# Four graph layers on one core: GpSimd copies the next chunk's gather indices a column at a time, between its own indirect DMAs

## The reference, cut to what matters

```python
def _gat_layer(x, src, dst, W, a_s, a_d, b, heads, outc):
    h = (x @ W).reshape(N, heads, outc)
    e = leaky_relu(alpha_s[src] + alpha_d[dst], 0.2)       # alpha_s needed at src of every edge
    p = exp(e - segment_max(e, dst)[dst])
    alpha = p / (segment_sum(p, dst)[dst] + 1e-16)
    return segment_sum(h[src] * alpha[:, :, None], dst) + b
x = layernorm(x + GAT(GAT(x)))           # two GAT layers: stages g1 and g2
x = layernorm(x + GCN(x))                # two GCN layers: stages c1 and c2
x = layernorm(x + sheaf(x))              # per edge an MLP of x[src], x[dst]; sums at src and at dst
x = layernorm(x + product(x))            # messages summed at src
```

## Time and profile before

| what | us |
|---|---|
| median of 3 runs | 38449.33 |
| the runs | 38229.62, 38449.33, 38707.31 |
| the profiled execution, its own time | 38408.23 |
| its span, first to last instruction | 38406.5 |

### The profile page before, as it was taken

The page is one execution under the profiler, slowest core; times in us unless marked ns, Lnnn a source line. Parts: engine busy times, 40 slices in busy tenths (PEclk is TensorE's granted clock), DMA queues, the critical chain, the costliest instruction groups (busy, mean ns, idle before and its releaser), DMA issues. The chain is left out here.

```text
span 38406.5 us, 266237 instructions
## 1 busy us (share of the span) xinstructions
PE 14357.5 (37%) x71326; PEld 10765.9 (28%) x71326; DVE 16060.9 (42%) x34560; ACT 2592.4 (7%) x3901; POOL 22432.8 (58%) x20450
## 2 busy tenths in 40 slices
PE   1111110111111047665566613433434344166664
PEld 1110000101010036554455612222223222044443
DVE  2332237223232546774566713332333344244443
ACT  0000000000000000000000000100101000033330
POOL 5777761355555256663676645755675665477773
PEclk5555555555555567776787856666666666577775
DMA  2011113111111311111111110000000000200001
GB/s 45 13 13 12 12 12 115 24 19 21 19 21 19 102 37 28 29 29 18 25 30 29 28 9 11 10 12 9 10 12 9 10 12 9 54 15 15 13 15 48
DMA packets 1089229, 935.10 MB, mean 24 GB/s; under 512 B 580668, under 2 KB 1031892, under 8 KB 1063892
## 3 DMA queue, kind: packets, MB, share of 16 engines
q1 hardware_dynamic: 440100, 695.25, 6.2%
q0 software_dynamic: 646368, 201.76, 6.1%
q10 hardware_dynamic: 1872, 28.29, 0.2%
HBM read 497.08 MB, written 426.83 MB: 24 GB/s over the span
## 5 line engine op out<-in xcount | busy, mean ns | idle before, releaser
L1139 POOL DMA_INDIRECT messages<-se_M,se_rstage x2625 | 3090.6, 1177 | 2987.9 <-DVE se_M L1502 2193.8
L1139 POOL DMA_INDIRECT messages<-pe_M,pe_rstage x2625 | 3131.6, 1193 | 1098.1 <-issue 791.8
L495 POOL DMA_INDIRECT g1g_G<-tab,g1g_stage x3125 | 3036.7, 972 | 1039.9 <-issue 1028.2
L495 POOL DMA_INDIRECT se_G<-tab,se_stage x3125 | 3036.6, 972 | 1039.9 <-issue 1026.2
L495 POOL DMA_INDIRECT g2g_G<-tab,g2g_stage x3125 | 2954.1, 945 | 1039.9 <-issue 1020.9
L495 POOL DMA_INDIRECT c1c_G<-tab,c1c_stage x2125 | 2473.0, 1164 | 658.9 <-issue 640.8
L495 POOL DMA_INDIRECT c2c_G<-tab16b,c2c_stage x2125 | 2457.1, 1156 | 658.9 <-issue 641.5
L1038 DVE SCALAR_TENSOR_TENSOR g2gh_junk<-g2gh_pB,g2gh_src_f,earlier 128x128 f32<-128x128 f32 (+4 forms) x2625 | 1459.0, 614 | 2804.2 <-remote 2136.7
L1447 DVE TENSOR_TENSOR se_V<-se_pTV,s_b 128x160 f32 (+1 forms) x625 | 202.8, 324 | 5740.6 <-remote 3207.6
L737 PE MATMUL g1gh_acc<-g1gh_oh_hi,g1gh_oh_lo 128*128 128x100 bf16 x6250 | 770.9, 272 | 4595.6 <-issue 3480.3
L1536 PE MATMUL se_pTV<-ident,se_pair 128*32 128x128 f32 x3125 | 585.9, 333 | 4058.2 <-DVE se_pair L1443 2428.0
(11 more groups left out here) (614 smaller groups left out, 34863.2 us busy)
## 6 DMA issues: line engine op xcount, KB each, us to landing
scans<-g1w_W SPq DMA_DIRECT2D x25, 3187.5 KB, 9.9
c1cm_row<-match SPq DMA_DIRECT2D x500, 128.0 KB
c2cm_row<-match SPq DMA_DIRECT2D x500, 128.0 KB
edges<-g2g_G SPq DMA_DIRECT2D x25, 2062.5 KB, 6.4
g2w_G<-edges SPq DMA_DIRECT2D x25, 2062.5 KB, 11.6
scans<-g2w_W SPq DMA_DIRECT2D x25, 2062.5 KB, 7.3
g1g_G<-tab,g1g_stage POOLq DMA_INDIRECT x3125
g2g_G<-tab,g2g_stage POOLq DMA_INDIRECT x3125
```

The costliest lines, as they stand in the source:

```text
L495: g.indirect_dma_start(out=G[b][:, t, :], out_offset=None, in_=table, in_offset=bass.IndirectOffsetOnAxis(ap=stage[b][:, t:t + 1], axis=0) ...
L1139: g.indirect_dma_start(out=view, in_=M[b][:, DC + t, :], in_offset=None, out_offset=bass.IndirectOffsetOnAxis(ap=stage[b][:, t:t + 1], axis=0)
```

## The change

`gat_gather` and `sheaf_edges` call a new function. While it issues the DMAs of chunk i from `stage[b]`, it fills `stage[1 - b]` with the indices of chunk i+1: from the sixth DMA on (AHEAD = 5), one copy of one column (of two columns in 5 of the 120) stands before each DMA. Before the first of these copies it waits until all DMAs of the last chunk have landed (`got[1 - b]`), because they read their indices from `stage[1 - b]`. At the start of a chunk it waits for the 120 copies on `staged[b]`. The first chunk's indices are staged by one copy (`stage_first`), the first chunk doesn't wait for a landing, and the last one stages nothing. The loops are cut so that the last two chunks (in `sheaf_edges` also the scatters around them) stand behind the loop. The order of gathers and scatters is the same.

```diff
+AHEAD = 5
+
+def stage_first(g, stage, staged, index, count=CH):
+
+    g.tensor_copy(stage[0][:, 0:count], index[:, 0:count]).then_inc(staged[0], count - AHEAD)
+
+def gather_and_stage(g, i, j, b, table, G, stage, staged, freed, credit, got, index, count=CH, begun=None, first=False,
+                     last=False):
+
+    g.wait_ge(freed[b], (j + 1) * credit)
+    g.wait_ge(staged[b], (j + 1) * (count - AHEAD))
+    g.nop(nofuse=True)
+    for t in range(count):
+        if t == AHEAD and not first and not last:
+            g.wait_ge(got[1 - b], (j + b) * (16 * count))
+            g.nop(nofuse=True)
+        if t >= AHEAD and not last:
+            n = count - AHEAD
+            start, stop = (t - AHEAD) * count // n, (t - AHEAD + 1) * count // n
+            g.tensor_copy(stage[1 - b][:, start:stop], index[:, bass.ds((i + 1) * CH + start, stop - start)]
+                          ).then_inc(staged[1 - b], 1)
+        if begun and t % GRP == 0:
+            g.sem_inc(begun, 1)
+        g.indirect_dma_start(out=G[b][:, t, :], out_offset=None, in_=table,
+                             in_offset=bass.IndirectOffsetOnAxis(ap=stage[b][:, t:t + 1], axis=0)
+                             ).then_inc(got[b], 16)
...
-                over_chunks(g, lambda i, b, j: gather_column_loop(
-                    g, k, i, j, b, table, G, stage, staged, stored, 32, got, k.src_i, begun=begun))
+                def chunk(i, b, j, first=False, last=False):
+                    gather_and_stage(g, i, j, b, table, G, stage, staged, stored, 32, got, k.src_i, begun=begun,
+                                     first=first, last=last)
+                stage_first(g, stage, staged, k.src_i)
+                chunk(0, 0, 0, first=True)
+                with g.Fori(0, PAIRS - 1) as j:
+                    chunk(2 * j + 1, 1, j)
+                    chunk(2 * j + 2, 0, j + 1)
+                chunk(NCH - 2, 1, PAIRS - 1)
+                chunk(NCH - 1, 0, PAIRS, last=True)
...
-                    gather_column_loop(g, k, i, j, b, table, G, stage, staged, free, 1, got, k.src_i)
+                def gather(i, b, j, first=False, last=False):
+                    gather_and_stage(g, i, j, b, table, G, stage, staged, free, 1, got, k.src_i, first=first, last=last)
...
-                gather(0, 0, 0)
-                with g.Fori(0, PAIRS) as j:
+                stage_first(g, stage, staged, k.src_i)
+                gather(0, 0, 0, first=True)
+                with g.Fori(0, PAIRS - 1) as j:
...
+                gather(NCH - 2, 1, PAIRS - 1)
+                scatter(NCH - 3, 0, PAIRS - 1)
+                gather(NCH - 1, 0, PAIRS, last=True)
+                release_messages(g, 0, PAIRS - 1, sent, mfree)
+                scatter(NCH - 2, 1, PAIRS - 1)
+                release_messages(g, 1, PAIRS - 1, sent, mfree)
                 scatter(NCH - 1, 0, PAIRS)
```

More of the change, by code:

```diff
@@ L1391, in _ @@
             def _(g):
-                def gather(i, b, j):
-                    gather_column_loop(g, k, i, j, b, table, G, stage, staged, free, 1, got, k.src_i)
+                def gather(i, b, j, first=False, last=False):
+                    gather_and_stage(g, i, j, b, table, G, stage, staged, free, 1, got, k.src_i, first=first, last=last)
                 def scatter(i, b, j):
```

## The result

| what | before | after |
|---|---|---|
| median, us (4 runs each) | 38482.83 | 36560.23 |
| the runs, us | 38229.62 to 38707.31 | 36275.78 to 36598.13 |
| span of the profiled execution, us | 38406.5 | 36520.8 |

The account below looks back on a forecast made before the run. It took GpSimd's indirect DMAs 1.25 us apart, starving the other engines, as the bound. 38408 - 776 (g2g) + 368 (g1g) - 1020 (se) = 36980, with 41 us from profiled execution to median: 37020 us; range 36200 to 38900.

Parts of the forecast that it names:

- The starvation, not the staging copy, is what the change can move: In g1g, g2g and se, other engines almost stand while GpSimd gathers; removing the staging copy gains only 0.3 us per chunk.
- (a): Rival: each new copy costs the DMA restart, 0.70 us, so the kernel takes 41530 us; chance 0.09.
- (c): Rival: the copy hides in the gap between DMAs (0 to 0.05 us), nothing is freed, about 38450 us; chance 0.09.
- (b): Rival: starvation stays at 1.45 us per DMA because the engines set GpSimd's pace; about 40400 us; chance 0.08.
- (d): Rival: the copy costs 0.10 us and a pace of 1.35 us is slow enough; 36100 us; chance 0.09.
- At 1.25 us apart starve the rest of the core, at 1.46 us they don't: Indirect DMAs' spacing decides starvation, read from c1c windows: PE did 32 matmuls in 106 us against 498 in 124.
- The copy, 0.20 us each: Each small copy before a gather DMA adds 0.20 us, making the pace 1.45 us per column; 9000 copies priced.
- g1g, +368 predicted: Stage g1g goes from 5377 to 5745 us: VectorE's runs hold copies, 9.0 us per five columns, 229 per chunk.
- g2g, -776 predicted: Stage g2g goes from 5401 to 4625 us: gathers of 184 us, GpSimd no longer waiting for a store.
- se, -1020 predicted: Stage se goes from 10221 to 9200 us: 25 cycles of 368 us, the gain all from the bad cycles.
- The landing wait, 0: GpSimd's new wait for the last chunk's DMAs to land costs 0; bound 0 to 4 us per chunk, 300 in all.
- Other stages, nothing: Other stages, cut-open loops and longer code cost nothing; bound 225 us for a second long gap per gather.

Follow-up runs that it names:

- B: A chip used for follow-up runs: the kernel before takes 40489 us there, the changed kernel 38542 us, ratio 0.955.
- staging ahead alone: Changed kernel with the next chunk's 125 indices staged in one copy before the sixth DMA, no small copies; on B 40589 us, ratio 1.002 to the kernel before.
- pace alone: Changed kernel with its small copies going into a buffer nobody reads, and staging as before the change; on B 37786 us, ratio 0.935 to the kernel before.
- the bunches: Changed kernel with its 120 small copies per chunk made 24 at a time before five of the DMAs; on C 36513 us, ratio 0.907 to the kernel before.
- A: The chip of the profiles before and after the change: the kernel before takes 38483 us there, ratio of the changed kernel 0.9465.
- D: A chip used for follow-up runs, without starvation: the kernel before takes 32858 us there; the changed kernel did not run on it.
- the kernel with one copy ahead: Changed kernel with the next chunk's indices staged in one 125-column copy before the sixth DMA; on D 32818 us, ratio 0.9988 to the kernel before.
- C: A chip used for follow-up runs: the kernel before takes 40269 us there, the changed kernel 37972 us, ratio 0.942.

## Why the prediction was right, point by point

- *The starvation, not the staging copy, is what the change can move*: right, and shown from both sides on B (staging ahead alone 1.002, pace alone 0.935). Rivals (a) and (c) are out, as DMAs come 1.41 us apart in g2g and 0.15 us behind a copy. Rival (b), that the starvation stays, is out by its numbers (waits near 48 us in g2g, 13 measured), but not as a whole: part of the starvation stays (matmuls 0.64 us apart, not 0.12). Rival (d), a copy of 0.10 us and 36100 us, is as near to the 36560 measured as the forecast. What the prediction couldn't know is that not every chip has the starvation: three of these five do.
- *"At 1.25 us apart starve the rest of the core, at 1.46 us they don't"*: the direction was right, the picture wrong. It isn't a pace that is either fast or slow enough; something fills up over some 20 us and drains in a pause (the bunches). At 1.41 us apart on A it fills up too: 28 to 36 us into a gather of g2g the matmuls come 1.4 us apart, as in the kernel before; what the kernel before has later in its gathers, 2.8 us apart, is nearly gone. And the windows of c1c couldn't decide it, as busy engines do slow GpSimd: on D, where nothing starves, a DMA of c1c takes 1.237 us against 0.944 in g2g, and they come 1.54 us apart.
- *The copy, 0.20 us each*: mis-sized. Undisturbed it costs 0.07 us, because half of the 0.30 us gap goes away behind it; the mean in g2g on A is (176.5 - 158.7) / 120 = 0.15, by moments in which GpSimd itself is late.
- *g1g, +368 predicted, -685 measured*: this is the step that failed, "this goes, but only until the sixth DMA, where the first new copy meets the same run", and with it "the copy after that is held to its end". The run of 61 us was starved work; at the new pace it doesn't arise. In what is left the copies are held for 0.5 us at a time: a group of five columns takes 186 / 25 = 7.4 us, not 9.0, and all waits between chunks go (215 us a chunk before, 186 after).
- *g2g, -776 predicted, -599 measured*: the gather is 176 us, not 184, but "GpSimd waits no more for a store" failed; 12 to 14 us remain, as VectorE does 1.16 instructions per us beside the gather, not the 2.2 that I took from the window without DMAs.
- *se, -1020 predicted, -610 measured*: same mistake. The copies are held little, as predicted (0.265 us on average), but the starvation is lifted only in part: 8 of 23 cycles are still slow (11 before), and 956.0 us of waiting for the messages remain where I had near 0.
- *The landing wait, 0*: right. *Other stages, nothing*: right (+44 us).
- *The sum*: that it came within 1.3% is luck in good part, as the errors cancel. Against 36980, g1g is 1053 less, g2g 177 and se 410 more: 36514, and the span is 36521. With g1g as forecast and the other two as measured it would have been 37567. Two slips of arithmetic move nothing: 25 cycles of 367 us are 9175, and 23 waits of 37 us are 851. The 1.33 us between DMAs of g1g, used for rival (b), is 1.30 on average (162.2 us for 125).
- The Trainium skill's rule (SBUF — State Buffer, section SBUF: two separate sides) that VectorE's lock also keeps a GpSimd DMA from writing its descriptors: the trace of before spoke against it, with 0.97 us on average. The DMA of 61.27 us on B shows that GpSimd can be held in full, and across 95 back-to-back instructions of VectorE, where the rule speaks of one; a run of 16 us in the changed kernel's g1g leaves DMAs at 1.0 to 1.4 us. What decides between the two is open.

## What to carry to other kernels

An engine that issues small DMAs without a break can slow all other engines of its core while it looks well used itself; look at how many instructions the others execute per us beside it and in its pauses, and check that they have work that they may do: in se on D VectorE executes only 0.38 per us beside a gather, because it soon has nothing left to do. Surer signs are instructions that wait for nothing and come far apart all the same. Where the others starve, a pause of about 5 us every 24 DMAs won more than the same copies spread out (0.907 against 0.942, on one chip). But try it on more than one chip: the same change gives 0.942 to 0.955 on three of these chips, and copies like its own cost 1 to 6% on a fourth.

## What the runs showed of the hardware that wasn't expected

- The kernel before takes 32858, 32998, 38483, 40269 and 40489 us on five chips, each within 2% of itself. TensorE's granted clock is much the same (0.652 on D, 0.628 on A, 0.618 on B). The stretches between the long gathers take equal times (1644 and 1176 us on B and D), though they hold 306 and 305 indirect DMAs each. The difference is in the stages with thousands of them, c1c and c2c too: 6760 us for both on D, 7943 to 9085 on A and B.
- The view of the DMA issues gives a median time from issue to landing on D and none on B, for the same code:

```profile
g1g_G<-tab,g1g_stage POOLq DMA_INDIRECT x3125
```

  on B, the kernel before, and on D, the kernel with one copy ahead:

```profile
g1g_G<-tab,g1g_stage POOLq DMA_INDIRECT x3125, 2.4
```

  The trace of B has too few records of semaphore updates by DMAs to match them: 98788 in all, against 348619 on D. The transfers themselves begin 1.7 us after a gather's first DMA starts and end 1.2 us after its last, in g2g on A and B.
- On the chips that starve a hand-over can take long even within one engine. In g2g on A, VectorE waits for the end of its own last instruction and for nothing else, and goes on 7.35 us later:

```profile
8949.34 0.08 DVE L1038 DVE_READ_ACCUMULATOR g2gh_junk<-g2gh_pB,g2gh_src_f,earlier 128x1 f32 x1
8956.78 0.40 DVE L1043 CAST rank<-cnt 128x5 f32 x1 [7.35 <-remote]
```

  Such waits inside the gathers of g2g take 2.99 us on average (up to 9.84) in the kernel before on A, 0.98 in the changed kernel, 0.68 in the bunched kernel on C, and 0.14 (up to 0.49) on D. This fits an overload of the way by which semaphore updates travel. But matmuls that wait for nothing are slow as well, so it can't be the waiting alone; what is overloaded is not shown. No run halved the number of updates per DMA, which would have told.
- An instruction of GpSimd that comes after a wait into a run of VectorE's fp32 to bf16 operations can be held to the run's end (a copy for 61.13 us, a DMA for 61.27 us), while a copy that followed directly on a DMA got in after 0.5 us.
